# Query and key stages of a gated attention layer in one block, with the weights kept on chip until they are rounded

## What is computed

```python
q = (layernorm(x) @ Wq + bq);  k, v = ctx @ Wkv + bkv     # 2048 queries, 4096 keys, 16 heads of 32
q, k = fq_sym(q * scale, axis=-1), fq_sym(k, axis=-1)     # round(x / s) * s, s = max|x| / 127
v = fq_sym(v, axis=keys)
attn = fq_unsigned(softmax(q @ k.T))
x = x + tanh(g_xattn) * ((attn @ v) @ Wp + bp)
x = x + tanh(g_ffn) * ffn(layernorm(x))                   # w = round(w / mean|w|) in -1..1, 512 -> 2048 -> 512
```

## Times and profile before

| | |
|---|---|
| median of 3 runs | 1773.95 us (1773.41 to 1774.96) |
| profiled execution | 1778.12 us, span 1776.3 us |
| busy share | PE 87%, DVE 92%, ACT 78%, POOL 73% |
| query stage, barrier, key stage | 0 to 82 us, to 91.8 us, to 259 us |
| attention's first instruction | 262.4 us |
| mean granted TensorE clock | 0.962 |

### The profile page before, as it was taken

One profiled execution on the slowest core, in us unless ns is written; L12 is line 12 of the kernel. 1 busy time (PEld: TensorE's weight loads), 2 busy tenths in 40 slices (PEclk: granted clock), 3 DMA queues, 4 the chain that ended last, 5 costly groups with the idle time before them and its releaser, 6 DMA issues.

```text
span 1776.3 us, 34679 instructions
## 1 busy us (share of the span) xinstructions
PE 1536.6 (87%) x13207; PEld 753.7 (42%) x13207; DVE 1629.8 (92%) x2214; ACT 1392.4 (78%) x1351; POOL 1297.2 (73%) x1297
## 2 busy tenths in 40 slices
PE   7799967888888888988888998988888887789996
PEld 4344422444444444444444444444444443333332
DVE  7869968999999999999999999999999999378887
ACT  4468867788898878889888888987887786677874
POOL 0156755889889989888998998898998898453322
PEclk9989987999999999999999999999999998799998
DMA  6769976999968999995898998688988967214233
GB/s 207 256 201 357 329 259 126 169 174 172 164 125 139 169 177 179 171 169 107 148 183 166 183 178 156 114 144 161 151 158 135 152 136 146 65 36 95 53 73 83
DMA packets 725640, 282.62 MB, mean 159 GB/s; under 512 B 676121, under 2 KB 680793, under 8 KB 724194
## 3 DMA queue, kind: packets, MB, share of 16 engines
q1 hardware_dynamic: 724098, 277.47, 75.7%
q0 software_dynamic: 704, 1.62, 0.3%
q10 hardware_dynamic: 672, 1.31, 0.2%
HBM read 76.59 MB, written 35.95 MB: 63 GB/s over the span
## 4 chain that ended last, share of the span: by engine, by line
DVE 34%; POOL 21%; PE 14%; issue 11%; ACT 3%; DMA 2%; POOLq 0%; SPq 0%; DVEq 0%; ACTq 0%
DVE att_scaled L1663 32%; POOL att_probsT L1395 17%; PE att_scores L1181 4%; PE att_ps_o L1201 3%; PE att_scores L1121 2%; POOL att_low_row L1385 2%; PE att_scores L1141 2%; DMA att_pairsT<-att_pairs 2%; ACT att_pairs L1261 1%; POOL att_bias_row L1388 1%; PE att_scores L1182 1%; DVE att_v_largest L1632 1%; PE att_scores L1083 1%; PE att_ps_v L1111 1%; PE att_ps_v L1201 0%
## 5 line engine op out<-in xcount | busy, mean ns | idle before, releaser
L1663 DVE TENSOR_SCALAR_CACHE_REDUCE att_scaled<-att_scores,layer_nsq 128x1536 f32<-128x1536 f32 (+1 forms) x768 | 1202.2, 1639 | 19.6 <-PE att_scores L1141 14.6
L1261 ACT ACTIVATE att_pairs<-att_scaled,att_bias_row 128x4096 uint8<-128x4096 f32 x256 | 950.4, 3713 | 141.8 <-DMA att_pairsT<-att_pairs 92.1
L1395 POOL CAST att_probsT<-att_pairsT 128x2048 bf16<-128x2048 uint8 x512 | 953.6, 1891 | 107.7 <-DMA att_pairsT<-att_pairs 97.3
L1141 PE MATMUL att_scores<-first_head_area 96*128 96x512 bf16 x1024 | 297.8, 396 | 95.9 <-DVE att_scaled L1663 79.6
L1141 PE MATMUL att_scores<-att_head_area 96*128 96x512 bf16 x1024 | 289.7, 385 | 65.4 <-DVE att_scaled L1663 62.6
L1102 PEld LDWEIGHTS att_ps_o<-att_v_head,att_probsT 128*128 128x128 bf16 x8192 | 242.9, 96 | 65.3 <-issue 3.0
L1102 PE MATMUL att_ps_o<-att_v_head,att_probsT 128*128 128x32 bf16 x8192 | 245.1, 177 | 2.8 <-DMA att_v_head<-layer_w2T 2.5
L1141 PEld LDWEIGHTS att_scores<-first_head_area 96*128 96x128 bf16 x1024 | 81.6, 99 | 257.0 <-DVE att_scaled L1663 174.9
L1141 PEld LDWEIGHTS att_scores<-att_head_area 96*128 96x128 bf16 x1024 | 80.0, 98 | 214.1 <-DVE att_scaled L1663 151.3
L1083 PE MATMUL att_scores<-att_head_area 96*128 96x512 bf16 x621 | 170.2, 384 | 0.0
L1083 PE MATMUL att_scores<-first_head_area 96*128 96x512 bf16 x570 | 158.4, 388 | 0.0
(11 more groups left out here) (181 smaller groups left out, 1599.8 us busy)
## 6 DMA issues: line engine op xcount, KB each, us to landing
layer_w2T<-ctx_T SPq DMA_DIRECT2D x96, 256.0 KB, 3.8
k_rows<-kv_parts SPq DMA_DIRECT2D x32, 392.0 KB, 4.1
q_w_in<-in_L_ffn_w_dram SPq DMA_DIRECT2D x32, 256.0 KB, 2.8
kv_weights_ctx_in<-in_ctx_dram SPq DMA_DIRECT2D x32, 256.0 KB, 4.8
kv_weights_w_in<-in_L_ffn_w_dram SPq DMA_DIRECT2D x32, 256.0 KB, 4.9
ctx_T<-kv_inT SPq DMA_DIRECT2D x8, 1024.0 KB, 6.6
q_x_in<-in_x_dram SPq DMA_DIRECT2D x16, 256.0 KB, 3.7
terns<-kv_tern SPq DMA_DIRECT2D x32, 128.0 KB, 4.5
```

Of the source, the lines that this page charges most:

```text
L1141: last = pe.matmul(buffer[:, x:x + 512], q_head[slot][:, at:at + P], k_head[slot][:, STARTS[j] + x:STARTS[j] + x + 512], start=True, stop= ...
L1261: act.activation(pairs[g % R_BUFS][:, :].bitcast(U8).rearrange("p (c two) -> p two c", two=2), scaled[u][:, :].rearrange("p (two c) -> p t ...
L1395: pool.tensor_copy(probsT[g % C_BUFS][:, parity * HALF:(parity + 1) * HALF, :].rearrange("p k q -> p (k q)"), bytes_now.rearrange("p (n tw ...
L1663: dve.tensor_scalar(scaled[u][:, STARTS[j]:STARTS[j] + WIDTHS[j]], scores[(g * NCH + j) % 2][:, 0:WIDTHS[j]], kept["nsq"][:, g:g + 1], Non ...
```

## The change

`project_queries` and `project_keys_values` become one function, `project`, in one block. There is one barrier less.

- All engines first run 18 query steps (Q_FULL). PE and ACT then alternate key steps 0, 1, 2 with the last query steps. DVE runs all 20 query steps first, then the key steps.
- The weight pieces go to 32 places on chip in the query stage (in `w2T`, in `o_sum` and in a new area) and stay there until ACT rounds them in the key stage, three steps behind instead of one. The second load is gone.
- Wk, its bias and three context tiles are loaded among the x tiles (after x tiles 8, 9, 11, 12, 13); a fourth context tile, the values' weights and bias follow the last pieces.
- Gates, Wq, its bias and the output bias are loaded from ACT's queue, gates first; Tanh is ACT's first activation. POOL splits b1 and gates the bias at the start.
- SP stores the last quarter of the queries and loads xb tile 0 before its key steps. An xb tile is loaded at step 2i-1, added at 2i, stored at 2i+1, in two buffers instead of four. The rounded tiles take the place of `q_stage`, the key parts that of Wq.

```diff
@@ SyncE
-                        after(sp, tern_ready, n - IN_BUFS + 1)
-                        sp.dma_start(w_in[n % IN_BUFS][:, :], piece).then_inc(w_loaded[n % IN_BUFS], 16)
-
-                    m = g - 2
+                    m = g - ROUND_LAG - 1
                     if live(m, KT):
                         sp.wait_ge(tern_ready, m + 1)
...
+                    i = row_tile(g, XB_STORE)
+                    if i is not None:
+                        sp.wait_ge(xb_ready, i + 1)
+                        sp.dma_start(xb_tiles[:, i, :], xb[i % XB_BUFS][:, :]).then_inc(xb_stored[i % XB_BUFS], 16)
                     i = row_tile(g, XB_LOAD)
                     if i is not None:
                         after(sp, xb_stored[i % XB_BUFS], 16 * (i // XB_BUFS))
                         sp.dma_start(xb[i % XB_BUFS][:, :], x_tiles[:, i, :]).then_inc(xb_loaded[i % XB_BUFS], 16)
...
+                for g in range(X_BUFS, QT):
+                    load_x(g)
+                    load_pieces(g - 2)
+                    if g in NEXT_AT:
+                        buffer, source, sem = next_loads[NEXT_AT.index(g)]
+                        sp.dma_start(buffer, source).then_inc(sem, 16)
+                for g in range(QT - 2, QT):
+                    load_pieces(g)
+                for buffer, source, sem in next_loads[len(NEXT_AT):]:
+                    sp.dma_start(buffer, source).then_inc(sem, 16)
                 sp.dma_start(kept["bv"][:, :], t["L0_xattn_bkv"][C:2 * C].rearrange("(k p) -> p k", p=P),
-                             allow_slow_non_contiguous=True).then_inc(gates_in, 16)
-                for a in range(3):
-                    sp.dma_start(q_first[a * D:(a + 1) * D, :], t["q_ints"][0, :, :]).then_inc(q_loaded, 16)
+                             allow_slow_non_contiguous=True).then_inc(weights_in, 16)
+                store_queries(sp, 3, last_q_stored)
+                sp.dma_start(xb[0][:, :], x_tiles[:, 0, :]).then_inc(xb_loaded[0], 16)
                 for g in range(STEPS + 1):
+                    if g == 4:
+                        sp.wait_ge(q_stored, 16 * 3 * (H // 4))
+                        sp.wait_ge(last_q_stored, 16 * (H // 4))
+                        for a in range(3):
+                            sp.dma_start(q_first[a * D:(a + 1) * D, :], t["q_ints"][0, :, :]).then_inc(q_loaded, 16)
                     step(g)
@@ TensorE
+                        if n < 2:
+                            pe.wait_ge(weights_in, 64)
+                            pe.wait_ge(q_math, QPER * (QT - 2 + n) + 1)
+                        else:
+                            pe.wait_ge(kv_math, NPER * (n - 2) + 1)
...
+                pe.wait_ge(q_const, 1)
+                for g in range(Q_FULL):
+                    query_step(g)
+                for g in range(3):
+                    step(g)
+                    query_step(Q_FULL + g)
+                for g in range(3, STEPS):
                     step(g)
@@ ScalarE
                 def round_weights(m):
-                    n = m % IN_BUFS
-                    act.wait_ge(w_loaded[n], 16 * (m // IN_BUFS + 1))
-                    act.activation(w_in[n][:, :], w_in[n][:, :], ACT.Identity,
+                    if m == 0:
+                        act.wait_ge(w_math, 2)
+                        act.wait_ge(q_stored, 16 * 3 * (H // 4))
+                        act.wait_ge(last_q_stored, 16 * (H // 4))
+                    act.activation(pieces[m], pieces[m], ACT.Identity,
                                    bias=up_down[:, 0:1], scale=kept["w_scale"][:, m % 2:m % 2 + 1]).then_inc(w_upped, 1)
...
-                    if live(g - 1, KT):
-                        round_weights(g - 1)
+                    if live(g - ROUND_LAG, KT - 1):
+                        round_weights(g - ROUND_LAG)
...
+                for i, name in enumerate(("g_xattn", "g_ffn")):
+                    act.dma_start(gates[:, i:i + 1], t[name].partition_broadcast(P)).then_inc(gates_in, 16)
+                act.dma_start(wq, t["L0_xattn_Wq"].rearrange("(k p) n -> p k n", p=P)).then_inc(q_weights_in, 16)
+                act.dma_start(bq[:, :], t["L0_xattn_bq"].partition_broadcast(P)).then_inc(q_weights_in, 16)
+                act.dma_start(bp[:, :], t["L0_xattn_bp"].partition_broadcast(P)).then_inc(gated_ready, 16)
+                act.wait_ge(gates_in, 32)
+                act.activation(kept["gate_tanh"][:, :], gates[:, :], ACT.Tanh).then_inc(gates_ready, 1)
...
+                for g in range(Q_FULL):
+                    query_step(g)
+                for g in range(3):
+                    step(g)
+                    query_step(Q_FULL + g)
+                query_step(Q_FULL + 3)
+                for g in range(3, STEPS):
                     step(g)
@@ GpSimd
+                pool.wait_ge(gates_ready, 1)
+                pool.wait_ge(gated_ready, 16)
+                pool.tensor_scalar(bp[:, :], bp[:, :], kept["gate_tanh"][:, 0:1], 0.0, ALU.mult, ALU.add).then_inc(gated_ready, 1)
                 split_bias()
+                for i in range(3):
+                    store_queries(pool, i, q_stored)
...
+                pool.wait_ge(total_ready, 1)
+                pool.partition_all_reduce(total_all[:, :], total[:, :], P, RADD).then_inc(total_all_ready, 1)
@@ VectorE
+                for g in range(QT + 4):
+                    query_step(g)
+                dve.wait_ge(w_summed, 2 * QT)
+                dve.tensor_reduce(total[:, :], sums[:, :, :], AX_X, ALU.add).then_inc(total_ready, 1)
...
+                for g in range(KT + 2):
                     step(g)
+                largest_values(KEY_BLOCKS - 1)
```

More of the change, by code:

```diff
@@ L50, in after @@
         eng.wait_ge(sem, value)
-def pipelined(eng, total, unroll, lag, step):
-    for g in range(total + lag):
-        step(g, g % unroll)
 def live(g, total):
@@ L492, in row_tile, with store_queries @@
             return i if (g - first) % 2 == 0 and 0 <= i < QT else None
+        def store_queries(eng, i, stored):
+            eng.wait_ge(q_kept, (i + 1) * QT // 4)
+            rows = slice(i * ROWS // 4, (i + 1) * ROWS // 4)
+            for g in range(H // 4):
+                eng.dma_start(t["q_ints"][4 * g:4 * g + 4, :, rows].rearrange("h d r -> (h d) r"),
+                              q_stage[:, g, rows]).then_inc(stored, 16)
         with nc.Block() as block:
@@ L497, in _, with load_x, load_pieces @@
             def _(sp):
+                def load_x(g):
+                    after(sp, xn_ready, g - X_BUFS + 1)
+                    sp.dma_start(x_in[g % X_BUFS][:, :], x_tiles[:, g, :]).then_inc(x_loaded[g % X_BUFS], 16)
+                def load_pieces(g):
+                    after(sp, w_summed, 2 * (g - 1))
+                    for m in (2 * g, 2 * g + 1):
+                        sp.dma_start(pieces[m], tile_and_piece(t, m)[1]).then_inc(a_loaded[g % 2], 16)
                 def step(g):
@@ L606, in step @@
                 def step(g):
[L608 to L610 removed]
                     j = (g - 8) // PER_BLOCK
[L613 removed]
+                    if g % PER_BLOCK == 0 and live(j, KEY_BLOCKS - 1):
+                        if j == 0:
+                            act.wait_ge(weights_in, 64)
                         keep_values(j)
```

492 lines of the change are left out of this document (216 added, 276 removed).

## The result

The kernel after takes 1768.63 us in the median of seven runs (1764.53 to 1774.66), the kernel before 1773.95 (1772.77 to 1776.89): 5.3 us less, a ratio of 0.9968 with an interval of 0.9955 to 0.9981. The profiled execution of after is the longest of its seven, 1774.66 us with a span of 1772.9, so that its attention stage must not be read as typical.

The account below looks back on a forecast made before the run. TensorE was taken to bound the key stage, leaving only the hole between stages to gain: -6.3 - 0.4 + 1.3 + 0.2 + 0.3 = -4.9 us from the 1773.95 median gives 1769.0 us, range 1764.0 to 1773.5.

Parts of the forecast that it names:

- What bounds the kernel, and the reloads worth nothing: Key stage: TensorE waits for nobody, so dropping 32 weight loads gains nothing; gain only in the hole between stages.
- Part 1: Seam, TensorE's order: key product 0 at 79.0 us, weights just in time, product 2 ending at 90.7; 18 us won so far.
- Part 2: Seam: key tile 4's load queues behind stores and xb; TensorE waits 8.3 us, product 4 at 107.5, gain 6.3 us.
- Rival C: Seam: the pause comes but the clock costs less, up to 2.9 us more gain, 1766.1 us; chance 0.12.
- Part 3: Key stage, rounding lag 3 and two xb buffers: pace unchanged (0); stage's end gains 0.4 us (0 to 0.9).
- Part 4: Activation tables: a new load before attention's first exponential comes on top, loss 1.3 us (0 to 1.3).
- Part 5: Start and query stage: gate loads and Tanh first cost 0.2 us, Wk among x loads 0.3 (0 to 1).
- B: Seam closes fully: TensorE never waits for key tile 4, gain 17.9 us, time 1757.4 us; chance 0.06.
- A: The forecast itself, 1769.0 us: key tile 4's load in series behind the xb tile; chance 0.60.
- D: Table switches cost more at the start and first exponential, +1.4 and +1.3 us: 1771.7 us, no change; chance 0.13.
- Rival E: Key stage: GpSimd paced by xb; landings over 7.0 us stop TensorE, at 7.6 us 1778 us, slower; chance 0.09.

Follow-up runs that it names:

- e7: Kernel before without the 28 reloads of feed-forward weight pieces in the key stage (weights then wrong); 1774.94 us, ratio 1.0006 to before.
- e2: Kernel after with xb tiles loaded, added and stored from key steps 3, 4, 5 on instead of -1, 0, 1; 1761.61 us (one run).
- e1: Kernel after with the loads of key tiles 4 to 6 issued before the last quarter's query stores; 1766.58 us (one run).
- e3: Kernel after with key tiles 4 to 6 loaded before the query stores and xb begun at key step 3; 1763.07 us, ratio 0.9915 to before.
- e4: Kernel after with Wk loaded as four 256 KB pieces behind x tiles 6 to 9; 1762.51 us, ratio 0.9931 to before.
- e8: Kernel after with each xb tile loaded in the key step that adds it, one step later; 1783.87 us (one run).
- e5: Kernel after with TensorE and ScalarE finishing all query steps before key step 0, not interleaved; 1764.65 us, ratio 0.9942 to before.
- e6: Kernel after with seven extra products of constants keeping TensorE busy in the pause before key transposes 4; 1773.85 us (one run).
- e10: Kernel after with two xb tiles and key tiles 4 to 6 loaded before the query stores, Wk in four pieces; 1755.53 us, ratio 0.9898 to before.
- e9: Kernel after with the edits of e3 and e4 together; 1760.03 us, ratio 0.9918 to before.
- e12: e10 with each xb add one key step later, behind that step's own sums; 1756.57 us, ratio 0.9897 to before.

## Why the prediction was right, and where it was not

The forecast of 1769.0 us stands against 1768.63 measured. The mechanism it rested on, key tile 4's load in series behind the xb tile, is there. Several of its terms were off, in opposite directions, and the trace shows them.

- **What bounds the kernel, and the reloads worth nothing:** right. TensorE's 4.73 us step is unchanged in after and in e7, which drops the reloads alone.
- **Part 1:** right in order. From the last query product, product 0 was forecast at +4.9 us and came at +5.47; 0.48 of that is a wait. The profile names ScalarE's copy as its releaser, but that had ended at 82.12. The small bias of the values was issued last, at 73.40, and landed 9.2 us later, at 82.6: TensorE waits for all these weights before product 0. In e2 the bias took 9.3 us and product 0 came at +5.57; in e1, e3 and e4 it landed in 5.9 to 7.9 us and product 0 came at +4.99 or +5.00. "Near, but in time" was off by half a microsecond.
- **Part 2:** right in mechanism, and near in size. Transposes 4 were forecast 24.9 us after the last query product and came 23.96 after it, product 4 at 33.4 against 31.99. Within the seam 7.7 us were won instead of 6.3; that the two are so close is in part luck, for the same stretch took 39.71 us in before and 36.81 in e7, and 31.99 in after, 31.17 in e4 and 29.70 in e8. The stores took 1.80 (forecast 1.7), the landing 2.8 (3.7), the add 1.26 (1.3). e1 to e3 confirm the cause by taking it away. e1 adds what the text had only as "beside it": GpSimd's chain stopped TensorE for 4.95 us as soon as the key tiles came early. And the forecast has no term for GpSimd behind its all-reduce, which e5 shows 1 us under the landing: it cost nothing here by that little.
- **Rival C's price** (2.9 us for the clock) was near: against e6, after paid 2.8, e4 and e8 2.3 and 1.5. The clock fell in all three.
- **Part 3:** the pace 0 was right, the tail's gain was mis-sized: 1.45 us, not 0.4 (above the bound of 0.9). Counted from the start of the last value products, the last k_rows issue ended at 14.67 us in before and at 13.81 in after, 0.86 earlier and not 0.4; and the xb store of 0.43 us behind it is gone, which the text names (0.45) but doesn't add.
- **Part 4:** wrong. The claim was that a table load begins only when its instruction's own wait is over. The first Sqrt of before bears it out (its load at 5.06 us, behind DVE's `mv`), the first exponential does not. There the load starts at 261.07, inside the idle ahead of the exponential: 1.28 of load and 1.09 of wait make 2.37 us, where before 2.38 us were idle. The cost is 0, not 1.3. Tanh shows the same at the start: its load at 3.46 us, ahead of the gates it waits for until 5.42. What tells the two cases apart is open. The Trainium skill ("ScalarE: Activation LUTs", What ACT_TABLE_LOAD costs) counts a drain of about 1.38 us beside the load's 1.28 at every switch; the load agrees with the row, and no drain shows in the time here.
- **Part 5:** wrong for Wk. I gave x tile 9 "about that much" slack without a row for it, and priced the step at 0.3 (0 to 1). DVE, which sets the query stage's pace, waited 2.85 us and the stage ended 3.1 us later, in the other six kernels with this load 1.1 to 3.0 later; e4 removes it wholly. That Wk delays what stands behind it on the queue by some 3 us was in the text; the slack was not there. The start's 0.2 was nearly so: the first raw sum came at 16.53 us, where it was 16.67.

In sum, from before to after at attention's start: seam 7.7, tail 1.45, query stage −3.1 makes 6.1 us, which is what the profiles show (262.46 to 256.38); the medians give 5.3. Forecast were 6.3 + 0.4 − 0.5 − 1.3 = 4.9. The errors of +1.4, +1.05 and +1.3 were nearly balanced by the −2.6 of Wk. So the time was met more closely than its terms deserve, and with single executions 2 to 3 us apart in the seam and in the query stage, the balance itself is no firmer than that.

One sum of the chances doesn't come out as written: B, C and three quarters of A make 0.63, not 0.66; the missing 0.03 is the part of D that isn't counted under "no change".

Rival E needed landings over 7.0 us; after's xb loads took 3.6 in the median. What stays open: the attention stage's length. In the profiled executions it was between 1507.3 (e8) and 1520.0 us (e6) from its first score product to the end, with the same instructions; before's was 1513.8 and after's 1516.5. That is most likely the larger part of the spread of 10 us among after's runs; only one of them has a profile, so it isn't shown. In after's trace such lost time stands, for example, behind a pair of DMA transposes whose issue took 6.74 us where the median of one is 1.99, but no run here tells what lengthens them.

```profile
1021.80 6.74 SPq L1030 DMA_TRANSPOSE att_pairsT<-att_pairs  x2
...
1028.86 3.71 ACT L1263 ACTIVATE att_pairs<-att_scaled,att_bias_row 128x4096 uint8<-128x4096 f32 x1 [3.40 <-DMA att_pairsT<-att_pairs]
```

## What to carry to other kernels

When a barrier between two stages falls, write out the queue that issues the transfers, not only the engine that computes: a load for the next stage that stands behind a wait for another engine is as good as a barrier. Moving five loads ahead of the stores shortened e10's way from the last query product to product 6 by 8.2 us against the kernel after, and Wk in pieces brings the last query product forward by 1 to 3 us more; the merge itself had given 5. Before a load is put among those of a running stage, look for the slack in a row of the engine that sets the pace, and split what is large to the size of its neighbours. And after each wait removed ask for the one under it: here SyncE's hid GpSimd's for the xb tile, that one hid GpSimd's behind the all-reduce, and that one another of SyncE's. Before the difference of two traces is given a cause, look in other kernels with the same code up to there for how much it varies by itself.

## What the runs showed of the hardware

- **GpSimd after an all-reduce.** The partition all-reduce shows as 0.41 us busy. The next instruction starts 7.11 (e10), 7.13 (e9), 7.62 (e12) and 7.69 us (e5) after its end, with no releaser in the trace. In all four it is a TENSOR_TENSOR. In before a CAST runs 11 us after the all-reduce, and the same idle time stands ahead of the first TENSOR_TENSOR (7.16 us in e7); so it may belong to the first of these after an all-reduce and not to the all-reduce's end, which no run separates. At the start of after, ahead of any all-reduce, a TENSOR_TENSOR follows a CAST at once (17.29 us). Most of the 5.5 to 6.6 us of idle time in front of the all-reduce is the wait for DVE's sum; from that sum's end to the all-reduce it was 1.2 to 2.6 us. (Spans on this engine are rough.)

```profile
95.30 0.19 POOL L656 CAST kv_b_parts<-kv_b_rest 128x16 bf16<-128x16 f32 x1 [2.31 <-DMA kv_b_rest<-in_L_ffn_b_dram]
102.60 0.20 POOL L659 TENSOR_TENSOR kv_b_rest<-kv_b_rest,kv_b_parts 128x16 f32<-128x16 f32 x1 [7.11 <-issue]
```

- **A table load can run ahead of its activation's wait,** and was then free where the activation waited for 1.28 us or more (261.07 and 3.46 us in after). It doesn't always: the load for the first Sqrt of before came at 5.06 us, right behind the operand that ended at 4.98.
- **A pause of 6.1 to 6.8 us costs more than its length:** 1.5 to 2.8 us for the lower clock behind it (after, e4, e8 against e6), and useless work in the pause buys that back. Behind pauses of 1.54 us (e2) and 0.66 us (e5) product 3 stayed at 3.60 us.
- **A small transfer behind large ones is late:** the 2 KB of the values' bias needed 9.2 us (2.2 on the empty queue of before), a 256 KB x tile behind the 1 MB of Wk about 9.1 (issued at 32.46, used at 41.59), against 4.7 in the median of its kind.
